# A two-layer graph network kernel: the upper half takes its two weights in turn, the last lift changes queue, and the node maxima are split

## The reference

```python
h = relu(layernorm(x))
# layer 0: edges 0..255 use W_hh, 256..1535 W_oo, 1536..8191 W_ho
feat  = concat([h[src], h[dst]], axis=1)          # all 8192 edges
e_f   = relu(feat @ W_kind + b_kind)
logit = e_f @ W_a + b_a
alpha = softmax of logit over the edges of one dst  # segment max, exp, segment sum
z     = segment_sum(alpha * h[src], dst)
x     = x + relu(concat([h, z]) @ W)                # W_hn for nodes 0..127, W_on for the rest
# layer 1
h     = relu(layernorm(x))
c     = edge_w * rsqrt(w_out[src] * w_in[dst])
agg   = degree-normed segment_sum(c * h[src], dst)
out   = x + relu(agg @ W_1 + b_1)
```

## Time and profile before

| | |
|---|---|
| runs shown | 601.23 us median of 3 (596.10 to 601.38) |
| profiled execution | 599.89 us, its span 597.4 us |
| busy: PE, DVE, ACT, POOL | 545.9, 418.6, 214.3, 172.4 us |
[...]
| transfers | 144.8 MB, mean 242 GB/s |

### The profile page before, as it was taken

One profiled execution on the slowest core, in us unless ns is written; L12 is line 12 of the kernel. 1 busy time (PEld: TensorE's weight loads), 2 busy tenths in 40 slices (PEclk: granted clock), 3 DMA queues, 4 the chain that ended last, 5 costly groups with the idle time before them and its releaser, 6 DMA issues.

```text
span 597.4 us, 7438 instructions
## 1 busy us (share of the span) xinstructions
PE 545.9 (91%) x2425; PEld 355.8 (60%) x2425; DVE 418.6 (70%) x744; ACT 214.3 (36%) x283; POOL 172.4 (29%) x163
## 2 busy tenths in 40 slices
PE   3999999999999998996399996898889999989996
PEld 2888888444444443432245454775657888868885
DVE  6999632588798789693986887666665276976234
ACT  3523434899455521000101192022524163224200
POOL 4014140477655735643473500000000001121000
PEclk9999999999999999899599995669997999989999
DMA  8956891899999999999799980040000656104002
GB/s 329 388 221 211 273 379 75 293 410 410 411 411 415 410 407 414 411 410 410 258 394 407 410 328 36 25 155 2 2 2 21 261 179 208 36 1 140 1 35 106
DMA packets 43492, 144.81 MB, mean 242 GB/s; under 512 B 5536, under 2 KB 5728, under 8 KB 43456
## 3 DMA queue, kind: packets, MB, share of 16 engines
q1 hardware_dynamic: 22000, 69.22, 31.0%
q0 software_dynamic: 19136, 69.22, 29.8%
q10 hardware_dynamic: 2320, 5.90, 2.6%
HBM read 131.70 MB, written 12.62 MB: 242 GB/s over the span
## 4 chain that ended last, share of the span: by engine, by line
PE 67%; DVE 16%; DMA 7%; issue 5%; POOL 1%; DVEq 1%; ACT 1%; ACTq 0%
PE banks L1089 23%; PE banks L1109 18%; PE banks L1251 7%; PE banks L1184 6%; DVE masked L796 4%; PE banks L1155 4%; PE banks L1268 4%; PE banks L1202 3%; DMA lift<-lift_row 3%; DVE rows L774 3%; DMA rows<-table,ids_i 2%; DVE rows L775 2%; DMA lift_row<-liftT 2%; DVE stats L676 1%; PE banks L1218 1%
## 5 line engine op out<-in xcount | busy, mean ns | idle before, releaser
L448 POOL DMA_INDIRECT rows<-table,ids_i x124 | 139.7, 1126 | 142.5 <-DVE rows L775 57.3
L1109 PE MATMUL banks<-w_raw,fT_raw 128*128 128x512 f32 x384 | 168.3, 599 | 7.6 <-DMA w_raw<-in_L_gnn_W_hn_dram 4.3
L1109 PEld LDWEIGHTS banks<-w_raw,fT_raw 128*128 128x128 f32 x384 | 73.0, 191 | 102.2 <-issue 89.4
L774 DVE TENSOR_TENSOR rows<-rows 128x1024 f32<-128x1024 f32 x62 | 75.7, 1222 | 35.3 <-DMA rows<-table,ids_i 27.8
L1089 PE MATMUL banks<-w_hi,fT_hi 128*128 128x512 f32 x200 | 78.1, 391 | 0.0
L686 DVE TENSOR_TENSOR w_lo<-w_raw,w_hi 128x1024 fp32r<-128x1024 f32 x40 | 48.3, 1224 | 42.2 <-ACT w_hi L497 37.1
L1089 PE MATMUL banks<-w_lo,fT_hi 128*128 128x512 f32 x200 | 77.8, 389 | 0.0
L1089 PE MATMUL banks<-w_hi,fT_lo 128*128 128x512 f32 x200 | 77.8, 389 | 0.0
L775 DVE SCALAR_TENSOR_TENSOR rows<-rows,wa_rep 128x1024 f32<-128x1024 f32 x62 | 75.9, 1225 | 2.1
L497 ACT ACTIVATE w_hi<-w_raw 128x1024 fp32r<-128x1024 f32 x40 | 41.7, 1056 | 78.3 <-PE banks L1089 63.8
L566 ACT ACTIVATE pick_src<-node_all,ids_f 128x512 f16<-128x512 f16 x64 | 42.7, 714 | 68.9 <-issue 34.5
(11 more groups left out here) (165 smaller groups left out, 643.7 us busy)
## 6 DMA issues: line engine op xcount, KB each, us to landing
w_raw<-in_L_gnn_W_ho_dram SPq DMA_DIRECT2D x16, 512.0 KB
table<-stage SPq DMA_DIRECT2D x32, 256.0 KB
w_raw<-in_L_gnn_W_oo_dram SPq DMA_DIRECT2D x16, 512.0 KB
w_raw<-in_L_gnn_W_on_dram SPq DMA_DIRECT2D x16, 512.0 KB
w_raw<-in_L_gnn_W_hn_dram SPq DMA_DIRECT2D x16, 512.0 KB
w_raw<-in_L_gnn_W_hh_dram SPq DMA_DIRECT2D x16, 512.0 KB
w_raw<-in_L_gnn_W_dram SPq DMA_DIRECT2D x8, 512.0 KB
lift<-lift_row ACTq DMA_DIRECT2D x7, 512.0 KB
```

Of the source, the lines that this page charges most:

```text
L448: pool.indirect_dma_start(out=rows[:, slot, side, :], out_offset=None, in_=table[kind][side], in_offset=bass.IndirectOffsetOnAxis(ap=ids_i ...
L774: step(dve.tensor_tensor(rows[:, r, 0, :], rows[:, r, 0, :], rows[:, r, 1, :], ALU.add))
L1109: ins = pe.matmul(bank[j][:, :], fT_raw[:, k, m * P:(m + 1) * P], w_raw[:, c % SLOTS, n * H:(n + 1) * H], start=(k == 0), stop=(k == K - 1))
```

## The change

1. Chunks 32 to 47 alternate: an even chunk is W_hn (banks 0 and 1), an odd one W_on (banks 2 to 7). DVE empties all eight banks in one go at c = 46. The waits of `bank_ready` follow.
2. The direct-edge logits and spread(0) (`hh_edges`, `spread`) stand at c = 61 of DVE's loop, ahead of tile rows 59 to 61. For that the two pick buffers swap places, and ACT waits for the last tile row before it copies the first span.
3. Lift 6 is sent and fetched by SP, behind load 67, as lift 7 is.
4. chunk_max(7) and `maxima` follow spread(4); `node_maxima` is done in four parts after spans 5, 6, 7 and 8; exponents, exp and split move to 9, 9 and 11; the last `degrees` to span 2.

```diff
-            q, k = (c - (C_BOT if bottom else C_TOP)) // K, c % K
+            q, k = ((c - C_BOT) // K, c % K) if bottom else (1 - (c - C_TOP) % 2, (c - C_TOP) // 2)
...
                 if j in (1, 7):
-                    eng.wait_ge(chunk_used, first + (2 * K if j == 1 else K))
+                    eng.wait_ge(chunk_used, first + 2 * K - (j == 1))
                 else:
-                    eng.wait_ge(bank_done, before + (j - 1 if j > 1 else 6))
+                    eng.wait_ge(bank_done, before + max(j, 1))
...
-        SEND_AFTER = (25, 29, 34, 39, 44, 54, 60)
-        FETCH_AFTER = (26, 30, 35, 40, 45, 55, 61)
+        SEND_AFTER = (25, 29, 34, 39, 44, 54)
+        FETCH_AFTER = (26, 30, 35, 40, 45, 55)
-        LAST_MAX, ME_PE, ME_DVE, PARTS, EXP = 3, 3, 5, 7, 3
+        LAST_MAX, ME_PE, ME_DVE, PARTS, EXP = 4, range(5, 9), 9, 11, 9
-        SP_LIFT = 7
+        SP_LIFT = 6
...
             act.wait_ge(hh_logits, TILE_HH)
+            act.wait_ge(edge_done, TE)
...
-                if c == C_TOP + 11:
+                if c == C_TOP + 14:
...
-                    keep_top(range(2, 8))
-                if c == C_HH + 3:
-                    keep_top(range(2))
+                    keep_top(range(8))
+                if c == C_BOT - 3:
+                    hh_edges()
+                    dve.wait_ge(hh_logits, TILE_HH)
+                    spread(0, w_col)
...
-                sp, slot = n % SPANS, n % 2
+                sp, slot = n % SPANS, (n + 1) % 2
...
             for k in range(K):
-                raw_chunk(C_TOP + k, k, range(2, 8))
-            for k in range(K):
-                raw_chunk(C_TOP + K + k, k, range(2))
+                raw_chunk(C_TOP + 2 * k, k, range(2))
+                raw_chunk(C_TOP + 2 * k + 1, k, range(2, 8))
...
-            def node_maxima():
+            def node_maxima(part):
 
                 pe.wait_ge(mpart_ready, 1)
-                for t in range(T):
+                for t in range(part * T // len(ME_PE), (part + 1) * T // len(ME_PE)):
...
-                ins.then_inc(me_done, 1)
+                if t == T - 1:
+                    ins.then_inc(me_done, 1)
...
-                if n == ME_PE:
+                if n == 2:
                     degrees(range(T // 4), closes=True)
-                if n == ME_PE:
-                    node_maxima()
+                if n in ME_PE:
+                    node_maxima(n - ME_PE[0])
```

More of the change, by code:

```diff
@@ L828, in whole_features, with spread @@
                                   fT_lo[:, k:k + 2, :].bitcast(F32), ALU.add).then_inc(fT_raw_done, 1)
+            def spread(n, col):
+                sp, slot = n % SPANS, (n + 1) % 2
+                if n >= 2:
+                    dve.wait_ge(span_full, n - 1)
+                first, extra = span_code(dve, words, n)
+                nodes = node_all[:, sp * SPAN:(sp + 1) * SPAN]
+                head = pick_dst[slot][:, 0:HEAD, :, :]
+                at_head = bass.ds(eng_first(dve, first), HEAD)
+                dve.tensor_tensor(head[:, :, 2, :], nodes[:, None, :].broadcast_to([P, HEAD, SPAN]),
+                                  dst_q[:, at_head, None].broadcast_to([P, HEAD, SPAN]), ALU.is_equal).then_inc(head_made, 1)
+                with dve.Fori(0, extra + 1) as i:
+                    q, at_pick = tile_no(dve, first + HEAD + i), tile_no(dve, i + HEAD)
+                    dve.tensor_tensor(pick_dst[slot][:, bass.ds(at_pick, 1), 2, :], nodes[:, None, :],
+                                      dst_q[:, bass.ds(q, 1), None].broadcast_to([P, 1, SPAN]), ALU.is_equal)
+                dve.memset(span_end[:, 2 * n:2 * n + 1], 0.0).then_inc(tail_made, 1)
+                dve.wait_ge(head_made, n + 1)
+                dve.tensor_tensor(head, head[:, :, 2:3, :].broadcast_to([P, HEAD, 3, SPAN]),
+                                  col[:, at_head, 1:4, None].broadcast_to([P, HEAD, 3, SPAN]), ALU.mult)
+                dve.wait_ge(tail_made, n + 1)
+                with dve.Fori(0, extra + 1) as i:
+                    q, at_pick = tile_no(dve, first + HEAD + i), tile_no(dve, i + HEAD)
+                    dve.tensor_tensor(pick_dst[slot][:, bass.ds(at_pick, 1), :, :],
+                                      pick_dst[slot][:, bass.ds(at_pick, 1), 2:3, :].broadcast_to([P, 1, 3, SPAN]),
+                                      col[:, bass.ds(q, 1), 1:4, None].broadcast_to([P, 1, 3, SPAN]), ALU.mult)
+                dve.memset(span_end[:, 2 * n + 1:2 * n + 2], 0.0).then_inc(span_ready, 1)
@@ new lines, in hh_edges @@
+            def hh_edges():
+                dve.wait_ge(bias_in[0], 48)
+                for r in range(TILE_HH):
+                    for n in range(2):
+                        bank_ready(dve, HH, 2 * r + n)
+                        ins = dve.tensor_tensor(h_edge[:, 0, r, n * H:(n + 1) * H], bank[2 * r + n][:, :],
+                                                bias[:, 0, n * H:(n + 1) * H], ALU.add)
+                    step(ins)
+                    dve.scalar_tensor_tensor(h_edge[:, 0, r, :], h_edge[:, 0, r, :], 0.0, wa_rep[:, :], ALU.max, ALU.mult,
+                                             accum_out=logit[:, TE + r:TE + r + 1]).then_inc(hh_logits, 1)
@@ L870, in _ @@
                     chunk_max(maxes[c])
-            def spread(n, col):
-                sp, slot = n % SPANS, n % 2
[L875 to L908, removed]
```

4 lines of the change are left out of this document (2 added, 2 removed).

## The result

| | before | after |
|---|---|---|
| median (lowest to highest) | 600.49 us (596.10 to 601.38), 4 runs | 604.67 us (603.66 to 610.53), 4 runs |
| ratio | 1 | 1.0121 [1.0076, 1.0165] |
| profiled execution, its span | 599.89, 597.4 us | 604.92, 603.0 us |
| mean granted clock | 0.945 | 0.943 |

The granted clock is a share of full speed. In windows of 1 us it reads 0.50 or 1.00 in both traces, and a value between only where it changes: before, 0.50 from 241 to 244 us, then 0.82, then 1.00 from 245 us.

A forecast was written before the change was run, and what follows sets the result against it. The prediction took the kernel as TensorE work with holes (67% of the chain). It summed 599.9 us + 4.2 (lift 7) + 4.0 (spans) = 608.1 us, stated as 608.5 us for the runs' offset, range 597 to 616 us.

The forecast's parts named there:

- The wait at chunk 36: Upper-half stage (chunks 32 to 47): TensorE waits 10.2 us at chunk 36 instead of 3.3, none later; stage ends at 282.8 us.
- The bank reads: Before W_hh: VectorE reads eight banks as TensorE frees them, to 283.6 us; TensorE's 8.32 us wait is gone.
- W_hh's start and end: W_hh stage: products begin at 288.8 us, 7.3 us sooner, and end 58.2 us later, at about 347 us.
- Lift 6 decides: Ahead of chunk_max(6): lift 6, sent behind load 67, is in at 359 us; VectorE stands 4.6 us, lift 7 +4.2 us.
- The gathers: Last tile rows: GpSimdE starts gathers 2 to 3.5 us later, yet rows 57 to 59 land within 2 us of before.
- The logits ahead of row 59: VectorE near W_hh's end: direct-edge logits (5.1 us) end at 350 us, filling a 2.0 us wait for gathers and no more.
- The spans: Lift 7 to the last layer's features: node maxima in parts and the clock cost +4.0 us.
- the low branch: Spans: clock stays low through the node-maxima parts, spans 5 to 8 take 5.9 us each, span 12 ends 6.5 us later.
- The offset to the median: Whole kernel: the runs' median lies above the profiled execution, so 608.1 us from the sum became 608.5 us.
- (c): Rival, chance 0.15: chunk 36 lands when wanted, no wait there; lift 7 -4.6 us, spans +0.4 us, 595.7 us.
- (b): Rival, chance 0.2: chunk 36 wait and late lift 6 as forecast, but the clock rises during the parts; about 605 us.
- (d): Rival, chance 0.2: no effect; W_hh's 7 us hidden, lift 6 costs 1 to 2 us, spans break even; 601 to 603 us.

## Why the prediction was right in size and partly wrong in cause
The forecast was 608.5 us, slower, in a range of 597 to 616 us; the time is 604.67 us, slower, with a ratio of 1.0121. That is under the 607.2 us from which the prediction would have called it clearly slower. The size is in part luck: lift 7 came late by another cause than the forecast one, and by the prediction's own sign of being wrong (lift 6 coming without a wait) its central step failed. Its parts:

- **The wait at chunk 36: right.** 10.2 us forecast, 9.04 us measured (9.04 to 11.61 us over six traces), none later; the stage ends at 283.4 us (282.8). The experiments with the load order show it: 4.46 us with four long chunks first, 1.15 us without the stores ahead, 15.85 us one ring turn later. The 282.8 us holds 1.7 us for the lower clock behind the wait, a term that no run shows by itself. What the runs show: before, the 60 records behind the wait took 27.71 us, 1.8 us more than at the 0.432 us each of the 51 ahead of it; after, the 96 took 44.30 us, 2.8 us more, with the clock at 0.50 in 240 to 244 us.
- **The bank reads: right.** VectorE waits 8.81 us from 268.7 us and no longer holds TensorE.
- **W_hh's start and end: too late, by 3.8 and 5.5 us.** I took 2.9 us of register loads and 3.1 us of transposes from the earlier trace rows. After, no such gap is left, and the transposes take 1.91 us. Then 58.2 us had 0.98 of the clock; after, it is 56.7 us at 1.00.
- **Lift 6 decides: wrong, and this is the step that failed.** The prediction had VectorE stand 4.6 us for it. SyncE could send it at 342.23 us, 5 us sooner than worked out, because W_hh ended sooner; and VectorE reached chunk_max(6) at 357.90 us, 3.5 us later than worked out, because the gathers were late. Two terms that were off by 5 and 3.5 us met in a difference of 4.6 us. Back on ScalarE's queue nothing changed. It does happen elsewhere: with W_hh's end at 351 us (bank reads two steps later) VectorE did stand 2.38 us for lift 6.
- **The gathers "land within 2 us of before": wrong, 5.0 us.** The start of GpSimdE's gathers 2 to 3.5 us later was nearly right (3.8 us); that it would be made up was not. This term, put at next to nothing, is what lift 7 paid: +4.2 us forecast, +3.2 us measured, with another cause.
- **The logits ahead of row 59: right in kind.** They fill VectorE's waits: 2.4 us of waits before, 0.3 us after row 58. Without the alternation they add 8.35 us of wait. By the ratios, parts 2 and 3 are worth -0.5% on top of the alternation (1.0033 against 1.0083; the intervals overlap) and +0.8% on top of the parts without it (1.0182 against 1.0104; the intervals just touch).
- **The spans: +4.0 us of +4.0, in part by luck.** Spans with parts take 5.96 us at 0.50, as in the low branch. Alone the split costs 1.0%. But the low branch came to +6.5 us at span 12 and the other to +0.4 us; +4.0 us was taken between them without a working. The clock then took a way between them too: it rose for some 7 us, from just ahead of the third part to behind the fourth, and fell again, and span 12 began 3.9 us later after lift 7.
- **What was left out:** the profiled execution is 604.92 us where the sum gave 608.1: 1.0 us of the 3.2 is lift 7, 1.6 us the tail, 0.6 us what lies around the span (1.9 us against 2.5). The offset to the median, +0.4 us forecast, was -0.25 us.

Of the rivals, a chunk 36 on time (c) did not come. (b), the clock rising during the parts, came for two of the four, and its 605 us is nearest to the time, but its terms (+4.2 and +0.4 us) are not those measured (+3.2, +4.0 and -1.6 us). (d), gains and losses that break even, was nearest in kind for lift 6, but not for the sum.

## What to carry over
A ring of slots must be judged where its queue is held up, not by its mean supply: count how long the slots loaded ahead last (in work, not in slots) against the landing of the first load behind a burst of stores (here TensorE ran out at 230.05 us, and that load was issued at 221.90 us and used at 239.09 us). When an engine's wait moves, follow it into the ring that this engine feeds; here a delay at a gather's start went round unshortened until the last tile rows (+3.8 us at row 48, +5.0 us at row 58). A difference of two times that are each worked out over 60 us should not decide a forecast; carry it with both ends instead.

## What the hardware showed that I had not expected
- The 2.9 us ahead of the transposes, where the program loads registers, stand in the three traces in which TensorE had waited for the last small chunks' weights (2.91, 2.91 and 2.88 us). In the kernel after, where matmuls ran up to them without a wait, the transposes follow with no gap (283.23 us). What fills the 2.9 us is not shown.
- TensorE was busy in every window and still held the lower clock in three traces: 0.50 from 392 to 400 us in the kernel after, from 372 to 400 us in the one with the maxima whole, from 384 to 388 us in the kernel before. The records there are 120-column picks, 40-column folds and 3-column maxima; the last take 27 ns each at 0.50 (256 in 6.99 us), and 27 ns (64 in 1.75 us) at 1.00 too, so the maxima lose next to nothing by the clock; the spans beside them do.
- Time and clock scatter together: over 77 executions of the kernel before, the fastest (594.53 us) had a mean granted clock of 0.960 and the slowest (606.10 us) 0.934, with a correlation of -0.82 (-0.77 without four of the slowest). Which of the two causes the other is not shown. A part of 4 us in the spans was settled by the ratios and by all traces together, not by a single one.
